# Three feed-forward streams written out step by step, with the experts' gates read back from DRAM

## What is computed

```python
# layer 1: weights rounded to -1, 0, 1; d_ff = 512
h = jax.nn.relu(jnp.einsum('bsd,fd->bsf', x, Wq1) + b1)
out = jnp.einsum('bsf,df->bsd', h, Wq2) + b2
# layer 2: 16 experts of width 64, grouped top-4 routing gives combine [tokens, 16]; one shared expert of width 128
g = jax.nn.silu(jnp.einsum('th,efh->tef', x, w1_e))
u = jnp.einsum('th,efh->tef', x, w3_e)
routed = jnp.einsum('tef,ehf,te->th', g * u, w2_e, combine)
# layer 3: 16 experts of width 128, top-4 softmax scores [tokens, 16]
gate = jnp.minimum(gu[..., ::2], LIMIT)
up = jnp.clip(gu[..., 1::2], -LIMIT, LIMIT)
act = (up + 1.0) * gate * jax.nn.sigmoid(gate * ALPHA)
out = jnp.einsum('te,teh->th', scores, jnp.einsum('tei,eih->teh', act, down_proj) + down_bias)
```

## Time and profile before

| | us |
|---|---|
| median of 3 runs | 1931.94 (1930.11 to 1936.6) |
| the profiled execution's own time | 1937.07 |
| its span, from the first to the last instruction | 1935.2 |
| TensorE matmuls busy | 1607.7 (83%) |
| VectorE / ScalarE / POOL busy | 1226.6 / 889.7 / 480.9 |
| mean granted TensorE clock | 0.895 |

### The profile page before, as it was taken

The page is one execution under the profiler, slowest core; times in us unless marked ns, Lnnn a source line. Parts: engine busy times, 40 slices in busy tenths (PEclk is TensorE's granted clock), DMA queues, the critical chain, the costliest instruction groups (busy, mean ns, idle before and its releaser), DMA issues. The chain is left out here.

```text
span 1935.2 us, 33277 instructions
## 1 busy us (share of the span) xinstructions
PE 1607.7 (83%) x12241; PEld 751.7 (39%) x12241; DVE 1226.6 (63%) x2588; ACT 889.7 (46%) x1711; POOL 480.9 (25%) x417
## 2 busy tenths in 40 slices
PE   5989736998888889877489888999569889899998
PEld 4665413343334344333234344333224344343333
DVE  4324667485567558344488887244668887268887
ACT  2331334676666666653256665321326665522221
POOL 1603266576676567300300000000200100000000
PEclk7989857999999999996689998799659999699999
DMA  7232267666676666301600100000430110000000
GB/s 209 92 82 71 59 202 191 168 164 175 161 195 159 164 173 173 93 1 44 168 19 19 35 19 1 1 0 0 125 98 22 31 33 5 1 0 1 0 0 22
DMA packets 211407, 153.63 MB, mean 79 GB/s; under 512 B 57600, under 2 KB 192184, under 8 KB 211128
## 3 DMA queue, kind: packets, MB, share of 16 engines
q1 hardware_dynamic: 201000, 134.90, 26.8%
q10 hardware_dynamic: 8208, 12.52, 2.2%
q0 software_dynamic: 2048, 4.20, 0.8%
HBM read 83.48 MB, written 67.37 MB: 78 GB/s over the span
## 5 line engine op out<-in xcount | busy, mean ns | idle before, releaser
L1938 DVE TENSOR_REDUCE a1a_partial<-a1a_room 128x4 f32<-128x1024 f32 x192 | 226.3, 1220 | 32.5 <-PE a1a_room L2003 31.9
L2378 ACT ACTIVATE a3a_probsT<-a3a_st 128x512 f32<-128x512 f32 (+2 forms) x320 | 155.9, 562 | 131.8 <-PE a3a_st L2444 76.8
L2378 ACT ACTIVATE a2a_probsT<-a2a_st 128x512 f32<-128x512 f32 (+2 forms) x320 | 155.7, 562 | 125.7 <-PE a2a_st L2444 73.6
L1897 ACT ACTIVATE a1a_probsT<-a1a_st 128x512 f32<-128x512 f32 (+1 forms) x416 | 204.9, 577 | 13.5 <-PE a1a_st L2036 12.2
L2290 DVE TENSOR_REDUCE a3a_maxima<-a3a_room 128x2 f32<-128x1024 f32 (+3 forms) x160 | 170.3, 1113 | 39.2 <-PE a3a_room L2413 25.3
L2290 DVE TENSOR_REDUCE a2a_maxima<-a2a_room 128x2 f32<-128x1024 f32 (+3 forms) x160 | 170.2, 1113 | 29.1 <-PE a2a_room L2413 19.1
L1802 POOL TENSOR_TENSOR a1a_shifted<-a1a_shifted,a1a_best 128x1024 f32<-128x1024 f32 x64 | 121.7, 1903 | 92.2 <-DVE a1a_best L1944 67.4
L2073 PE MATMUL a1a_ctx<-a1a_probsT,a1a_vpad 128*9 128x512 f32 (+3 forms) x1408 | 140.6, 498 | 0.8
L1934 DVE CUSTOM_DVE_ANT_0 a1a_shifted<-a1a_room,a1a_bands 128x256 f32<-128x256 f32 x256 | 93.3, 421 | 74.6 <-PE a1a_room L2003 67.3
L2003 PE MATMUL a1a_room<-stack 48*128 48x128 bf16 (+1 forms) x1376 | 107.4, 260 | 36.7 <-DVE a1a_partial L1938 19.3
L2036 PE MATMUL a1a_st<-stack 51*128 51x512 bf16 (+3 forms) x576 | 116.3, 316 | 20.5 <-ACT a1a_nearT L1904 6.4
(11 more groups left out here) (500 smaller groups left out, 3224.5 us busy)
## 6 DMA issues: line engine op xcount, KB each, us to landing
a1a_bands<-a_band SPq DMA_DIRECT2D x112, 192.0 KB, 3.9
a_near<-a1a_shifted SPq DMA_DIRECT2D x112, 192.0 KB, 3.0
a1a_near<-a_near SPq DMA_DIRECT2D x64, 256.0 KB, 4.1
a_band<-a1a_r_mix SPq DMA_DIRECT2D x64, 254.0 KB, 3.7
stack<-q SPq DMA_DIRECT2D x96, 96.0 KB
stack<-k SPq DMA_DIRECT2D x32, 96.0 KB
l_inputs<-l_zeros SPq DMA_DIRECT2D x1, 2624.0 KB, 11.1
q<-a1j_parts ACTq DMA_DIRECT2D x10, 256.0 KB, 3.1
```

Source lines behind the costliest of these rows:

```text
L1897: nc.scalar.activation(dst, src, ACT.Exp).then_inc(exp_done, 1)
L1938: nc.vector.tensor_reduce(partial[:, g % 2, :, 1 + r].rearrange("p (a s) -> p a s", a=2), src, X_AXIS, ALU.max).then_inc(job_free, 1)
L2378: nc.scalar.activation(probsT[:, block_at % BLOCK_ROOMS, place:place + heads, lo:], src, ACT.Exp).then_inc(exp_done, 1)
```

## The change

`Stream`, `run_stream` and `split3` go. Each of the three stages is now written out without loops, so that waits compare with constants, and TensorE issues two steps ahead, with three buffers of a, b and `hid`, and two of y (one in the ternary stage). The gate matmul goes. The routers turn the fp32 gates only, keep them as [16, tokens] in `gateT`, and SP stores that to DRAM at the end of the attention stage; the feed-forward stages read each gate row back from DRAM, spread over the partitions, into four buffers (`GateRows`): in the grouped stage two transfers a tile, one an expert, for 64 partitions each. In the clamped stage the clamp of the gate half moves from VectorE to ScalarE: 7 - relu(7 - bias - a), with the subtraction folded into Silu's scale and bias. The ternary stage's Sqrt moves behind the second chunk.

The diff, cut to its core:

```diff
 # ternary_ffn
+        N, AHEAD, NORM_AFTER = NCH * C, 2, 1
+        a, y, hid = [ph.ps(f"a{i}") for i in range(3)], ph.ps("y"), ph.sb("hid", [P, 3, CHUNK])
...
+                def up(n):
+                    c, j = divmod(n, C)
+                    if n >= 3:
+                        pe.wait_ge(hid_ready, n - 2)
+                    nc.tensor.matmul(a[n % 3][:], w1T[:, j, :], k.xnT[:, c * CHUNK:(c + 1) * CHUNK], start=True, stop=True).then_inc(up_done, 1)
...
+                for n in range(N):
+                    c, j = divmod(n, C)
+                    if n + AHEAD < N:
+                        up(n + AHEAD)
+                    if j == 0 and c:
+                        pe.wait_ge(y_read, c)
+                    pe.wait_ge(hid_ready, n + 1)
+                    nc.tensor.matmul(y[:], w2T[:, j, :], hid[:, n % 3, :], start=(j == 0), stop=(j == C - 1)).then_inc(hid_used, 1)
...
+                for n in range(N):
+                    c, j = divmod(n, C)
+                    act.wait_ge(up_done, n + 1)
+                    if n >= 3:
+                        act.wait_ge(hid_used, n - 2)
+                    nc.scalar.activation(hid[:, n % 3, :], a[n % 3][:], ACT.Relu, bias=b1[:, j:j + 1]).then_inc(hid_ready, 1)
+                    if c and j == AHEAD - 1:
+                        gates_of(c - 1)
+                        if c - 1 == NORM_AFTER:
+                            deviation()
+                gates_of(NCH - 1)
 # TailRouter
-        self.parts = ph.sb("r_parts", [P, NT, 3 * self.E], BF16)
-        k.gateT = ph.sb("gateT", [3 * self.E, TOK], BF16)
+        self.gateT = ph.sb("r_gateT", [self.E, TOK])
+        self.dram = nc.dram_tensor(self.ROWS, [self.E, TOK], F32).ap()
...
+            mm = self.nc.tensor.transpose(dst[0:self.E, t * P:(t + 1) * P], self.tile["gates"][:, half * NT // 2 + t, :], self.k.ident[:])
...
+    def store(self, sp, job_free, count):
+
+        sp.wait_ge(job_free, count)
+        sp.dma_start(self.dram, self.gateT[:]).then_inc(self.stored, 16)
+        sp.wait_ge(self.stored, 16)
+class GateRows:
+    KEPT = 4
+    def load(self, sp, m, srcs, hid_ready, read_by):
+        if m >= self.KEPT:
+            sp.wait_ge(hid_ready, read_by)
+        n = P // len(srcs)
+        for i, src in enumerate(srcs):
+            sp.dma_start(self.tile[i * n:(i + 1) * n, m % self.KEPT, :], src.broadcast_to([n, CHUNK])).then_inc(self.landed[m % self.KEPT], 16)
+    def wait(self, dve, m, parts):
+        dve.wait_ge(self.landed[m % self.KEPT], 16 * parts * (m // self.KEPT + 1))
 # GroupRouter, SoftmaxRouter
-    PE_NS, DVE_NS, CHAIN_NS = 4 * [1800.0] + [3800.0] + 2 * [900.0], 4 * [1300.0] + [500.0] + 2 * [1300.0], 4 * [0.0] + [37000.0] + 2 * [0.0]
+    PE_NS, DVE_NS, CHAIN_NS = 4 * [1800.0] + [3800.0] + 2 * [1800.0], 4 * [1300.0] + [500.0] + 2 * [1300.0], 4 * [0.0] + [37000.0] + 2 * [0.0]
-    JOBS, WIDTH = 5, 32
+    JOBS, WIDTH, ROWS = 3, 32, "l3_gates"
 # grouped_ffn
+                for m in range(NCH * M):
+                    c, j = divmod(m, M)
+                    c0, j0 = divmod(m - rows.KEPT, M)
+                    srcs = [r.dram[e:e + 1, c * CHUNK:(c + 1) * CHUNK] for e in (2 * j, 2 * j + 1)]
+                    rows.load(sp, m, srcs, hid_ready, c0 * J + j0 + 1)
...
+                    nc.vector.tensor_tensor(mid[:, n % 2, :], b[n % 3][:], acted[:, n % 3, :], ALU.mult).then_inc(mid_ready, 1)
+                    dve.wait_ge(mid_ready, n + 1)
+                    rows.wait(dve, c * M + j, 2)
+                    if n >= 3:
+                        dve.wait_ge(hid_used, n - 2)
+                    nc.vector.tensor_tensor(hid[:, n % 3, :], mid[:, n % 2, :], rows.of(c * M + j), ALU.mult).then_inc(hid_ready, 1)
 # clamped_ffn
+                    rows.load(sp, n, [r.dram[j:j + 1, c * CHUNK:(c + 1) * CHUNK]], hid_ready, n - rows.KEPT + 1)
...
+                    if n >= 3:
+                        pe.wait_ge(below_ready, n - 2)
+                    nc.tensor.matmul(a[n % 3][:], r.each[:, 0, j, :], x, start=True, stop=True).then_inc(a_done, 1)
+                    if n >= 3:
+                        pe.wait_ge(linear_ready, n - 2)
+                    nc.tensor.matmul(b[n % 3][:], r.each[:, 1, j, :], x, start=True, stop=True).then_inc(b_done, 1)
...
+                def room_below(n):
+                    j = n % E
+                    act.wait_ge(a_done, n + 1)
+                    if n >= 2:
+                        act.wait_ge(act_ready, n - 1)
+                    nc.scalar.activation(below[:, n % 2, :], a[n % 3][:], ACT.Relu, bias=r.gate_room[:, j:j + 1], scale=-1.0).then_inc(below_ready, 1)
...
+                room_below(0)
+                for n in range(N):
+                    c, j = divmod(n, E)
+                    if n + 1 < N:
+                        room_below(n + 1)
+                    act.wait_ge(below_ready, n + 1)
+                    if n >= 3:
+                        act.wait_ge(mid_ready, n - 2)
+                    nc.scalar.activation(acted[:, n % 3, :], below[:, n % 2, :], ACT.Silu, bias=r.top[:, 0:1], scale=-SLOPE).then_inc(act_ready, 1)
+                    if c and j == AHEAD:
+                        gates_of(c - 1)
...
+                    nc.vector.scalar_tensor_tensor(out=hid[:, n % 3, :], in0=mid[:, n % 2, :], scalar=1.0 / SLOPE, in1=rows.of(n),
+                                                   op0=ALU.mult, op1=ALU.mult).then_inc(hid_ready, 1)
 # causal_attention, SyncE
+                router.store(sp, job_free, jobs.index(("router", 0, router.JOBS - 1)) + 1)
                 sp.wait_ge(rows_in, 64 * UNITS)
```

More of the change, by code:

```diff
@@ L855, in run_stream @@
[L855 to L861, removed]
-        @block.scalar
-        def _(act):
-            stream.scalar(act)
-        if stream.b:
-            @block.vector
-            def _(dve):
-                stream.vector(dve)
 def expert_weights(nc, ph, w):
@@ L1093, in deviation, with gates_of @@
                     nc.scalar.activation(std[:], std[:], ACT.Sqrt).then_inc(std_ready, 1)
-                stream.scalar(act, deviation)
+                def gates_of(c):
+                    act.wait_ge(hid_used, C * (c + 1))
+                    nc.scalar.activation(k.gT[:, c * CHUNK:(c + 1) * CHUNK], y[:], ACT.Silu, bias=b2[:, 0:1]).then_inc(y_read, 1)
+                for n in range(N):
[9 more added lines that the diff above has]
+                gates_of(NCH - 1)
             @block.vector
@@ L1175, in scalar, with turn_gates @@
         self.nc.scalar.activation(score[:], score[:], ACT.Exp).then_inc(self.exp_done, 1)
-    def turn_parts(self, pe, dst, half):
-        pe.wait_ge(self.split, 1)
+    def turn_gates(self, pe, dst, half):
+        pe.wait_ge(self.gated, 1)
         for t in range(NT // 2):
-            mm = self.nc.tensor.matmul(dst[0:3 * self.E, t * P:(t + 1) * P], self.parts[:, half * NT // 2 + t, :], self.k.ident_bf[:], start=True, stop=True)
+            mm = self.nc.tensor.transpose(dst[0:self.E, t * P:(t + 1) * P], self.tile["gates"][:, half * NT // 2 + t, :], self.k.ident[:])
@@ L1181, in turn_parts, with keep_gates @@
         return mm
-    def keep_parts(self, src, half):
-        return self.nc.vector.tensor_copy(self.k.gateT[:, half * TOK // 2:(half + 1) * TOK // 2], src[0:3 * self.E, :])
-    def split_gates(self, chain):
-        split3(self.nc, chain, self.tile["gates"][:], [self.parts[:, :, self.E * i:self.E * (i + 1)] for i in range(3)], self.tile["rest"][:])
-        chain.mark(self.split)
+    def keep_gates(self, src, half):
+        return self.nc.vector.tensor_copy(self.gateT[:, half * TOK // 2:(half + 1) * TOK // 2], src[0:self.E, :])
@@ new lines, in store, with __init__, of @@
+    def store(self, sp, job_free, count):
[4 more added lines that the diff above has]
+    KEPT = 4
+    def __init__(self, nc, ph):
+        self.tile = ph.sb("rows", [P, self.KEPT, CHUNK])
+        self.landed = [ph.sem(f"rows{i}") for i in range(self.KEPT)]
+    def of(self, m):
+        return self.tile[:, m % self.KEPT, :]
+    def load(self, sp, m, srcs, hid_ready, read_by):
[6 more added lines that the diff above has]
+        dve.wait_ge(self.landed[m % self.KEPT], 16 * parts * (m // self.KEPT + 1))
@@ L1242, in vector @@
             chain = Chain(dve, self.steps)
[L1243 removed]
+            dve.wait_ge(self.filled, 1)
             dve.wait_ge(self.exp_done, 1)
@@ L1335, in vector @@
             chain(nc.vector.tensor_tensor(gates[:], gates[:], over(self.red[:], 2, E), ALU.mult))
-            self.split_gates(chain)
+            chain.mark(self.gated)
 def grouped_weights(nc, ph, w):
```

290 lines of the change are left out of this document (134 added, 156 removed).

## The result

The changed kernel took 1861.4 us (median of 4 runs, 1859.9 to 1866.7) where the kernel before took 1934.3 beside it (4 runs, 1930.1 to 1939.2): a ratio of 0.963, interval 0.960 to 0.966. The profiled execution took 1859.92, span 1858.0, clock 0.903. The forecast was 1857.9, in 1848 to 1882. Of all the runs reported here one, of the version with two edits near the end, took 1917.2 us at a granted clock of 0.815 where its others had 0.89 to 0.90, and its median and ratio leave it out.

What follows compares the result with a forecast made beforehand. TensorE and VectorE were taken to bind the clamped step together. Ternary -9.9, grouped -19.8, clamped -43.7 and router ends -0.6 sum to -74.0, taking the median from 1931.94 to 1857.9 us, range 1848 to 1882.

Steps and rivals of the forecast that it cites:

- Both engines bind together: Old clamped step of 3.09 us: TensorE full, VectorE nearly as full at 2.87, so each must lose one operation.
- The two waits in the earlier trace: Old clamped step: `f_gated` waits for f_g and f_y for `f_hid`, cited with both engines binding together.
- dropping only the matmul would leave VectorE at 2.9: Clamped step: without the gate matmul alone, VectorE's four operations would still take 2.9 us.
- Ternary stage: Ternary feed-forward stage: unrolled, with fewer table loads, 31.2 us against 41.1, -9.9, bounds -8 to -11.
- Grouped stage: Grouped feed-forward stage: 108 matmuls at 0.86 and the last Silu, 93.7 us against 113.5, -19.8, bounds -17 to -21.
- Clamped stage: Clamped feed-forward stage: 2.58 us a step plus bias matmuls and ends, 172.5 us against 216.2, -43.7, bounds -35 to -46.
- slack of 0.4: Clamped step: chain through Relu, Silu, mid and hid ends at 4.8 us, before TensorE's y(n) at 5.2.
- The clamp's price: Clamped stage: ScalarE's Relu at 686 ns against 742 on VectorE, so moving the clamp fits despite the skill's advice.
- Rival A: Both gated stages: gate rows arrive at only 80 to 96 GB/s, total 1872 to 1925 us; chance 12%.
- Rival B: Silu's table lacks Relu, so every clamped step loads two tables: stage +43.4, total 1947 us; chance 4%.
- Rival C: Clamped step's latencies exceed the 0.4 to spare; at 2.8 us a step the total is 1872 us; chance 14%.
- Router ends: Ends of the two attention stages: +1.0 for fp32 transposes, -1.6 for dropped jobs, -0.6 in all, bounds -6 to +6.

Runs made afterwards that it cites:

- the version with two edits near the end: Changed kernel with ScalarE doing each clamped step's Relu and Silu together, and two banks each of a and y in the ternary stage: median 1857.4 us, ratio 0.957.

## Why the prediction was right, and where it was off

The measured 1861.4 lies 3.5 above the forecast of 1857.9, and the gain is 72.9 by medians and 77.2 by the two profiled spans, for 74.0. In the profiles the clamped stage gained 1.7 less than forecast and the ends 4.9 more; that these errors have opposite signs is luck.

**Both engines bind together: half right.** TensorE alone set the old step: put back alone, the gate matmul restores its 3.09 exactly. VectorE stood 0.32 behind: with its four operations it needs 2.77 and then is the bound, so both had to lose one for 2.58, as forecast. The two waits in the earlier trace rows were read as proof that both bind, but `f_gated` waits there for TensorE, and the wait of `f_y`'s weights for `f_hid` cost nothing. The size for VectorE was off as well: "dropping only the matmul would leave VectorE at 2.9" gives 2.77 when measured. I added up durations of records, of which two overlap the next by 0.08.

**Ternary stage, 31.2 forecast, 31.28.** The stall at two of three inner ends was 1.22 and the return behind it 0.1 (forecast 1.36), the Sqrt with its load was hidden behind the four matmuls, and Relu loaded no table. Of the gain of 9.8, 1.7 goes with the lower clock (0.96) of the one profile of before that the forecast was read from; it did not weigh that.

**Grouped stage, 93.7 forecast, 93.58.** 108 x 0.86 and the last Silu; VectorE's 2.4 us of waiting for the first rows cost nothing, as TensorE never waited. The gate matmul was not put back in this stage; at the clamped stage's 0.51 the 32 of it would be 16.3 of the 19.9, an estimate.

**Clamped stage, 172.5 forecast, 174.15.** The step was right to 0.01; of its slack of 0.4 only 0.27 is there, because the load of `f_y`'s weights and the step from `f_hid` to it were left out. Three terms of the ends were mis-sized: the start 1.2 where I had 0.7 (the Relu of step 1 stands ahead of the first Silu, and its table is loaded only then), the last matmuls and Silu 3.5 for 3.3, and the change from 128 to 16 rows and back at three chunk ends, 1.2, was left out.

**The clamp's price.** `f_below` took 687 ns and the clamp on VectorE 745 in the experiment. The rule of the page ScalarE: Activation LUTs (Rules for kernel authors) of the Trainium skill sends relu to VectorE; the trace was right to decide against it. With the clamp on VectorE the stage is 8.7 us longer, because VectorE is then the bound. Silu with its bias took 711 ns where I allowed 690 at most; ScalarE had the room.

**Rival A, rows too slow,** was a real mechanism with a wrong limit. I took 80 and 96 GB/s as possible ceilings from a stretch in which few transfers were in flight; asked for twice the rows, the kernel got 163, against 102 wanted by the change. Its argument against itself ("the engines were idle two thirds of that time") was unsound too, for at 163 the share is 0.88. What could have made the rows too slow was the form of the transfer, which I had not weighed: one transfer a tile would have done it in the grouped stage.

**Rival B, tables alternate,** did not happen: one load in the clamped stage. The Trainium skill (ScalarE: Activation LUTs, Table sets: the hidden batching unit) says that relu is in every set. The trace agrees: no Relu in the three stages loaded one.

**Rival C, latency,** did not happen, but by 0.27 us in two steps. One step ahead with the same order shows it at work: 4.88 a step, and up to 6.6 where the clock fell.

**Router ends, -0.6 forecast** within 6: -5.5 in the two profiles compared (the head and the tail of the program among them), of which the clamped attention is 4.1. Here the forecast was wrong in size, inside its bounds. In the clamped attention about 2 go to the jobs (1.6 forecast), 0.5 to a loop head that the forecast put at nothing, and the rest goes with the clock.

## What to carry to other kernels

When two engines fill a step almost equally, price the removal from each alone, and read an engine's pace from the starts of its records, since sums of durations overstate it. Write a broadcast from DRAM so that its slowest dimension is long (one transfer per row, not one for two rows), and take its rate from a run with the real number in flight. With a long chain behind an in-order engine, the order of that engine's instructions can be worth a whole step of look-ahead.

## What had not been expected

- Transfers that each read one DRAM row of 2 KB for all partitions stopped at 163 GB/s, at a DMA share of 0.88, where twice 102 was asked for; with half of the bytes from other rows 198 to 201 passed at 0.63 to 0.66. The busy share of the DMA engines is therefore no measure of what is left: 0.33 at 99 GB/s stood for three fifths of that ceiling, not a third.
- In the run with one step ahead, where a chain kept TensorE waiting in every step, 28 of 62 steps had matmuls at the 1.2 GHz level (mean granted clock 0.86): the stage took 346 us where the chain at full clock, worked out beforehand, gave 313.
- A matmul of 16 rows between two of 128 rows cost 0.4 us more than its place in the pace, at each of three chunk ends.
